# Mask waits of the key and value gathers replaced by landing waits

## What is computed

```python
kv_scores, indices = _pk(x, Wq_pk, pk_keys)          # 16 slots for each token and head
ind = indices + offsets[None, None, :, None]
k = jnp.einsum('bnhk,bnhkd->bnhd', kv_scores, keys_table[ind])
v = jnp.einsum('bnhk,bnhkd->bnhd', kv_scores, values_table[ind])
sim = jnp.einsum('bihd,bjhd->bhij', q, k)            # then causal softmax, times v, times Wo
```

## Time and profile before

| | us |
|---|---|
| median of the runs | 3272.53 |
| span of the profiled execution | 3918.3 |
| its part before the first gather of the mixer | 348.5 |
| from the first to the end of the last gather | 3345.7 |
| its part after the last gather | 224.1 |
| PE, DVE, ACT, POOL busy in the span | 3008.9, 2785.8, 2039.4, 2057.7 |

### The profile page before, as it was taken

How to read it: one execution, slowest core, us unless ns; L and a number is a source line. 1 busy time by engine, 2 the same in 40 slices (tenths; PEclk the granted TensorE clock), 3 DMA queues, 4 the chain that set the end, 5 groups by cost and what they waited for, 6 DMA issues and landing times.

```text
span 3918.3 us, 39268 instructions
## 1 busy us (share of the span) xinstructions
PE 3008.9 (77%) x9722; PEld 1391.1 (36%) x9722; DVE 2785.8 (71%) x9999; ACT 2039.4 (52%) x4498; POOL 2057.7 (53%) x2095
## 2 busy tenths in 40 slices
PE   4861657878787878878778868888778878888888
PEld 2430223333333333333333433333333433333343
DVE  7678777777777777776777887777768786874433
ACT  3231545555555555655555655556555655555532
POOL 3011666666656665555565655556656655655400
PEclk8985777888787888989888989888888988989899
DMA  1001121212121111112121212111111212121100
GB/s 37 22 8 52 44 66 43 62 45 57 48 56 47 52 52 50 52 46 55 44 59 38 65 40 57 44 52 53 51 50 46 57 46 56 42 62 39 33 3 3
DMA packets 85626, 179.86 MB, mean 46 GB/s; under 512 B 40177, under 2 KB 41107, under 8 KB 85398
## 3 DMA queue, kind: packets, MB, share of 16 engines
q0 software_dynamic: 66560, 135.40, 13.1%
q1 hardware_dynamic: 18838, 41.94, 3.5%
HBM read 176.15 MB, written 1.05 MB: 45 GB/s over the span
## 4 chain that ended last, share of the span: by engine, by line
PE 41%; DVE 25%; another core or an unknown queue 11%; issue 8%; ACT 8%; ACTq 0%; DVEq 0%
PE mx_acc L1430 12%; PE mx_O L1442 7%; PE mx_area L1476 6%; DVE mx_W L1787 5%; PE mx_D L1420 4%; ACT mx_GT L1691 3%; DVE mx_KVs L2013 3%; PE mx_area L1456 2%; ACT mx_W L1623 2%; DVE mx_mx_part L2031 2%; PE mx_area L1492 1%; DVE mx_mx L2031 1%; PE mx_X L1560 1%; PE mx_area L1486 1%
## 5 line engine op out<-in xcount | busy, mean ns | idle before, releaser
L1402 POOL DMA_INDIRECT mx_G<-in_kv_table,mx_slot_i x2048 | 2004.0, 978 | 1394.6 <-issue 590.1
L1430 PE MATMUL mx_acc<-mx_W,mx_table 128*128 128x512 f32 x2048 | 1180.7, 660 | 1.6 <-ACT mx_kvT L1630 0.7
L1787 DVE SCALAR_TENSOR_TENSOR mx_W<-mx_D,mx_W 128x512 f32<-128x512 f32 x1024 | 699.1, 683 | 297.5 <-ACT mx_W L1623 180.5
L1623 ACT ACTIVATE mx_W<-mx_D 128x512 f32<-128x512 f32 x1024 | 606.6, 593 | 523.2 <-PE mx_D L1420 231.0
L1691 ACT ACTIVATE mx_GT<-mx_G,mx_slot_w 128x128 f32<-128x128 f32 x2048 | 759.2, 495 | 3.2 <-DVE mx_KVs L2013 1.1
L1420 PE MATMUL mx_D<-mx_U,mx_pick_b 96*128 96x512 bf16 x1024 | 432.7, 423 | 110.8 <-DVE mx_W L1787 52.5
L1430 PEld LDWEIGHTS mx_acc<-mx_W,mx_table 128*128 128x128 f32 x2048 | 436.1, 214 | 201.9 <-issue 104.5
L1647 ACT ACTIVATE mx_PT<-mx_area 128x512 f32<-128x512 f32 x472 | 241.8, 514 | 464.9 <-PE mx_area L1480 146.3
L1442 PE MATMUL mx_O<-mx_PT,mx_KVs 128*65 128x512 f32 (+3 forms) x768 | 347.5, 536 | 170.0 <-ACT mx_PT L1647 82.8
L1456 PE MATMUL mx_area<-mx_KTa,mx_QTa 64*128 64x512 f32 (+3 forms) x384 | 200.6, 607 | 132.6 <-DVE mx_mx L2031 66.1
L2013 DVE TENSOR_REDUCE mx_KVs<-mx_GT 128x128 f32<-128x2048 f32 x128 | 291.9, 2280 | 6.0 <-ACT mx_GT L1691 5.9
(11 more groups left out here) (390 smaller groups left out, 4462.4 us busy)
## 6 DMA issues: line engine op xcount, KB each, us to landing
mx_table<-in_kv_dense SPq DMA_DIRECT2D x64, 512.0 KB
mx_G<-in_kv_table,mx_slot_i POOLq DMA_INDIRECT x2048
tz_table<-in_c_dft SPq DMA_DIRECT2D x1, 2048.0 KB
tz_table<-in_c_idft SPq DMA_DIRECT2D x8, 256.0 KB, 2.6
out_h<-mx_xc SPq DMA_DIRECT2D x4, 256.0 KB
mx_G<-in_c_pick SPq DMA_DIRECT2D x1, 528.0 KB
st_h<-in_tok_W,em_ids POOLq DMA_INDIRECT x32
st_keys<-in_pk_keys SPq DMA_DIRECT2D x1, 512.0 KB, 3.9
```

Of the source, the lines that this page charges most:

```text
L1402: pool.indirect_dma_start(G[g % RING][:, r, :], None, a["kv_table"], bass.IndirectOffsetOnAxis(slot_i[n % 2][:, k, r:r + 1], 0))\
L1430: pe.matmul(acc[:, :], table[:, tile, :], W[c % TILE_RING][:, :], start=(tile == 0), stop=(tile == TILES - 1)).then_inc(applied, 1)
L1623: act.activation(W[c % TILE_RING][:, :], D_ps[c % 3][:, :], ACT.Exp).then_inc(p_done, 1)
L1787: dve.scalar_tensor_tensor(W[c % TILE_RING][:, :], D_ps[c % 3][:, :], 0.0, W[c % TILE_RING][:, :], ALU.is_ge, ALU.mult).then_inc(w_done, 1)
```

## The change

The wait for masks is taken out. Instead, before gathers 0, 4, 8 and 12 of each group, POOL waits until every gather issued so far has landed: before gather 0 on the full count of the group before, in the other buffer's semaphore, and before the others on the count of its own group so far. The very first gather has no such wait. All other waits, the order of the gathers and the buffers stay.

```diff
 RING = 2
+LANDED = 4
 TILE_RING = 6
@@
                 if g >= RING:
                     pool.wait_ge(scaled, g - RING + 1)
                 for r in range(TOPK):
-                    ahead = SLOT * n + 8 * k - 6 + r // 2
-                    if r % 2 == 0 and ahead > 0:
-                        pool.wait_ge(w_done, ahead)
+                    if r % LANDED == 0 and (g or r):
+                        before = NB * n + k - (r == 0)
+                        pool.wait_ge(gathered[before % RING], 16 * (TOPK * (before // RING) + (r or TOPK)))
                     pool.indirect_dma_start(G[g % RING][:, r, :], None, a["kv_table"],
                                             bass.IndirectOffsetOnAxis(slot_i[n % 2][:, k, r:r + 1], 0))\
                         .then_inc(gathered[g % RING], 16)
```

## The result

The changed kernel takes 4078.88 us (median), against 3271.78 us for the kernel before beside it: a ratio of 1.2467, 95% interval 1.2439 to 1.2495. The forecast was 3690 us with a range up to 3790. The direction and the place were right, and the size was half of what came.

A forecast was written before the change was run, and what follows sets the result against it. The prediction took the pipeline of scores, exponential and mask to bound the kernel before, and POOL's gather chain after the change: 478 us outside plus 128 groups x 25.1 us gives 3691, so 3690 us, range 3270 to 3790.

The forecast's parts named there:

- the things to look for: Changed kernel's profile: no mask waits, some 511 landing waits of about 1.6 us, many ScalarE landing waits, span 3920 to 4050.
- The nothing for the mask waits: POOL's 546.6 us of idle time at mask waits, removed by the change, was costed at nothing.
- The gathers do not set it.: Kernel before: scores, exponential and mask set the pace, with holes; ScalarE waited once for a landing, 1.1 us.
- one ratio: Median over profiled span, 0.835, applied to the gather stretch (2794 us) and to the rest (478 us).
- 1.4 us to spare in a group: POOL before the change: 20.4 us of gathers and spacing against a timed group of 21.8 us.
- The landing wait: On POOL, four a group: 1.59 us each from issue end to next start, in place of 0.30.
- the sum by it, 3490 us: Alternative sum with the skill page's 2.15 us per waited gather: 23.5 us a group, about 3490 us.
- The bound with the mean duration, 25.6: POOL's group length with the mean gather of 0.978 us: 25.6 us, giving 3755 us for the kernel.
- The part outside: Time outside the gather stretch: 572.6 us profiled, taken as 478 us in a timed run.
- POOL's spacing did not shrink without a profile: Rival: POOL's times shrink fully in timed runs, 21.0 us a group, time stays 3272; 0.16 with the wait doing nothing.
- a partial shrink: Rival: POOL's times shrink partly in timed runs, giving 3294 to 3600 us; chance 0.14.
- The faster case: Rival: mask waits already held ScalarE up; removing them gives back up to 179 us, 3093 at best; chance 0.08.

The follow-up runs named there:

- the disturbed execution: The profiled execution of the unchanged kernel before that the prediction read: span 3918.3 us.
- profiled again: The kernel before, no edit, profiled once more: 3266.51 us, ratio 1.0008, span 3263.3 us.
- the kernel with eight waits: The changed kernel with a landing wait before every second gather, eight a group in place of four: 4891.83 us, ratio 1.4961.

## Why the prediction was right in kind and wrong in size

**Right:** the mask waits cost next to nothing; the landing waits lay the latency open; POOL's chain of gathers becomes the period; ScalarE then stands at its wait for the landing. Of the things to look for, the mask waits are gone, the landing waits number 510 (511 were named), and ScalarE's waits rose to 127. The profiled span should have moved far less than the runs, to 4050 us at most; instead span and runs agree in both kernels, 4082.0 and 4078.9, 3263.3 and 3266.5.

The nothing for the mask waits was right with some luck. The prediction's reason was that ScalarE had waited for gathers only once. It had waited 60 times, 224.8 us in all. What made the price nothing is that POOL, let go by the masks (86.7 us), met the buffers later (67.8 us for 27.3): its idle time only fell from 770.9 to 762.6 us.

**Wrong: "The gathers do not set it."** The prediction rested it on one wait of 1.1 us and on POOL's waits for masks. In the execution profiled there, the pipeline had holes that the timed runs don't have, and so the gathers had room. The prediction saw the holes, took them out of the sum with one ratio, and then left POOL 1.4 us to spare in a group. The ratio of span to median said that this profile couldn't tell which engine waits for which in a timed run; the sum of 20.4 us on POOL against 21.8 us was the only warning, and it was read as slack. The runs show 0.5 us of it: the wait at a group's first gather is worth 262 us among four and costs 202 us alone. This step was wrong about the kernel before, but it does not enter the forecast, which takes POOL's chain as the period in any case. What put the number out are the terms of that chain.

**The terms of the sum.** Forecast 478 + 128 x 25.1 = 3691; measured 554 + 128 x 27.6 = 4082 by the profile.

- The landing wait: 1.59 us, taken from a waiter on ScalarE. On POOL a wait opens a gap of 1.8 us when it rides on the gather and 2.3 when it needs an instruction of its own, 2.04 in the mean. Four of them make 8.2 us for 6.4: 1.8 x 128 = 230 us. This is the largest miss, and the step that failed. The row itself was a fair one: in the changed kernel, too, ScalarE starts 1.59 us after the group's last issue ended, in the median. But ScalarE starts 0.02 us after the last landing and POOL 0.26 us, or 0.76 us behind a separate wait. The price was carried from one engine to another without POOL's own start, which makes up 0.36 of the 0.45 us by which a wait was too cheap. The rest is landings that came later, 1.66 us after the issue in the mean, where 1.57 us lie behind the row. The Trainium skill, "DMA: Bandwidth & Descriptors", section "Anatomy of one DMA — SWDGE (gpsimd) path", has the fixed price as mostly completion. The trace does not agree: at the gather shown, 0.70 us pass from the end of the issue to the first packet, and 0.33 us from the last packet to the last landing. The figure of about 2.0 us is short of the 0.94 + 1.8 = 2.7 us that a waiting POOL pays here from issue to issue, so the sum by it, 3490 us, falls further short than the forecast.
- The gather: 0.966 us in the mean (1979.17 / 2048), where the median of 0.944 was taken: 16 x 0.022 x 128 = 45 us. The spacing without a wait was 505.7 / 1537 = 0.33 for 0.30: 12 x 0.03 x 128 = 46 us. Most of that is not a longer spacing, but 18 stops of 2.25 us at the second gather of every seventh group. The bound with the mean duration, 25.6, was the better value.
- The part outside: 334.3 + 219.9 = 554 us for 478. The ratio was applied to it, but the disturbed execution was only 14 us longer before its first gather and 14 us after its last (348.5 and 224.1 us, for 334.8 and 209.9 when profiled again): 76 us.

Together 397 us, and 3691 + 397 = 4088, 6 us from the span. The range fell short at its upper end because that end took the same 1.59 us as certain, from the single place where a row showed it on another engine.

**The rivals.** POOL's spacing did not shrink without a profile, and a partial shrink didn't come either: the median gather is 944 ns in both profiles of the kernel before. The faster case had half of its mechanism right: ScalarE did stand waiting before the change, but taking the masks away gave nothing back (ratio 0.9993).

## What to carry to other kernels

When an engine's own work nearly fills the period, a wait for the landing of its newest transfer is paid nearly in full each time: here 0.5 us a group was covered. Wait for an older one, so that the latency lies under the issues that follow. And when a profile's span is far from the timed runs, take the profile again before asking which engine has slack: the holes that lengthened it also give slack to engines that have none.

## What the runs showed of the hardware

- A gather on POOL carries one wait at no cost when it is met (3262.98 us with 381 more of them, 3262.95 without). A second wait on the same gather becomes a semaphore instruction; where it ends a delay, the gather starts 0.76 us after the landing and not 0.26 (gaps of 2.27 and 1.79 us).
- POOL needs more time than ScalarE to start after a landing: 0.26 us against 0.02 in the changed kernel, or 1.79 us after the issue ended against 1.59.
- A gather of 64 KB lands some 2.5 us after its issue starts (median of the kernel with eight waits), of which POOL is busy for 0.94.
- The matmuls of the gather stretch (8376 records, and 8375 before) took PE 2625 us at a mean granted clock of 0.85, and 2396 us at 0.94 before the change. TensorE stood at the lower of its two levels for 1271 us of the changed kernel's execution and for 472 us of the one before. PE idled more in between, but that this brought the lower level on is not shown. With 4% of the chain on PE, it can have cost little here.
